# A software-pipelined transformer block on one core: the order of two stages within a step, where they overlap

## The reference

```python
x = x + tanh(g_xattn[0]) * cross_attention_0(layernorm(x), ctx)        # 16 heads of 8, causal
x = x + tanh(g_ffn[0]) * local_transformer(layernorm(x))
x = x + tanh(g_xattn[1]) * cross_attention_1(layernorm(x), ctx)
x = x + tanh(g_ffn[1]) * experts(layernorm(x))                          # top 2 of 8

# local_transformer, twice:
h = shift_token(x); q, k, v = split(h @ wqkv)          # 8 heads of 64, windows of 64
q, k = rotary(l2norm(q) * qs), rotary(l2norm(k) * ks)
x = x + local_attention(q, k, v) @ wo
h = layernorm(shift_token(x)) * lg + lb
a, g = split(h @ w1 + b1)
x = x + (a * gelu(g)) @ w2 + b2
```

## Time and profile before

| what | value |
|---|---|
| median of 3 runs | 1270.78 us (1269.67 to 1273.89) |
| the profiled execution, its own time | 1272.81 us |
| its span | 1270.9 us |
| mean granted clock of PE | 0.96 |

### The profile page before, as it was taken

How to read it: one execution, slowest core, us unless ns; L and a number is a source line. 1 busy time by engine, 2 the same in 40 slices (tenths; PEclk the granted TensorE clock), 3 DMA queues, 4 the chain that set the end, 5 groups by cost and what they waited for, 6 DMA issues and landing times.

```text
span 1270.9 us, 34469 instructions
## 1 busy us (share of the span) xinstructions
PE 1166.9 (92%) x11848; PEld 983.7 (77%) x11848; DVE 1026.1 (81%) x2368; ACT 955.8 (75%) x2545; POOL 859.6 (68%) x1110
## 2 busy tenths in 40 slices
PE   7788976799999998887999999989889998999997
PEld 4377764588888878875888888789767776999997
DVE  3299985899999975677999999858878886688887
ACT  2299984799999985446999999865588986666664
POOL 6188873899999983338999999833576762334332
PEclk8699997999999999998999999999989999999999
DMA  6000000000000001210001200001000000000000
GB/s 181 1 2 2 2 10 7 10 11 10 10 11 10 13 4 23 62 27 8 11 11 27 60 11 13 4 19 31 13 1 1 2 1 2 8 14 13 14 14 13
DMA packets 56555, 21.74 MB, mean 17 GB/s; under 512 B 44689, under 2 KB 54975, under 8 KB 56386
## 3 DMA queue, kind: packets, MB, share of 16 engines
q1 hardware_dynamic: 55154, 19.22, 6.2%
q10 hardware_dynamic: 1232, 0.33, 0.1%
HBM read 9.06 MB, written 2.10 MB: 9 GB/s over the span
## 4 chain that ended last, share of the span: by engine, by line
PE 71%; ACT 8%; DVE 7%; issue 7%; POOL 4%; SPq 1%; DMA 1%; ACTq 0%; DVEq 0%; POOLq 0%
PE m_ps_h L1401 7%; PE m_ps_y L1413 7%; PE a_ps_s L902 5%; PE a_ps_b L994 5%; PE a_ps_t L1005 5%; PE a_ps_t L969 4%; PE a_ps_a L929 4%; PE a_ps_qk L886 3%; PE x_ps_t L575 3%; PE a_ps_s L941 2%; ACT x_khm L636 2%; PE a_ps_qk L888 2%; PE a_ps_qk L887 2%; PE x_ps_s L531 2%; PE f_ps_g L1269 2%
## 5 line engine op out<-in xcount | busy, mean ns | idle before, releaser
L1057 ACT ACTIVATE a_e<-a_ps_s,a_stat 128x128 f32<-128x128 f32 x512 | 226.7, 477 | 4.5 <-DVE a_stat L1126 4.4
L1192 POOL TENSOR_TENSOR a_stat<-a_stat,small 128x16 f32<-128x16 f32 x64 | 187.2, 2925 | 5.3
L1182 POOL TENSOR_TENSOR a_e<-a_e,a_stat 128x1024 f32<-128x1024 f32 x64 | 121.2, 1893 | 8.3 <-DVE a_stat L1105 8.3
L1057 ACT ACTIVATION_READ_ACCUMULATOR a_e<-a_ps_s,a_stat 128x1 f32 x512 | 115.8, 226 | 0.0
L729 DVE TENSOR_REDUCE x_stat<-x_ps_s 128x16 f32<-128x1024 f32 x64 | 78.3, 1224 | 41.2 <-PE x_ps_s L532 41.2
L1299 ACT ACTIVATE f_gl<-f_ps_g,vec 128x128 f32<-128x128 f32 (+1 forms) x192 | 55.8, 361 | 59.7 <-PE f_ps_g L1269 59.6
L1401 PE MATMUL m_ps_h<-m_hT,w 128*128 128x128 f32 x768 | 96.1, 283 | 0.0
L1200 POOL TENSOR_TENSOR a_rot<-a_rot,a_stat 128x512 f32<-128x512 f32 x64 | 90.1, 1407 | 5.0
L1413 PE MATMUL m_ps_y<-w,m_up 128*128 128x128 f32 x768 | 91.1, 275 | 1.5 <-DVE m_yw L1448 1.5
L1401 PEld LDWEIGHTS m_ps_h<-m_hT,w 128*128 128x128 f32 x768 | 90.8, 196 | 0.0
L1434 ACT ACTIVATE m_up<-m_ps_h 128x512 f32<-128x512 f32 x96 | 57.1, 598 | 43.5 <-PE m_ps_h L1401 43.5
(11 more groups left out here) (182 smaller groups left out, 3782.1 us busy)
## 6 DMA issues: line engine op xcount, KB each, us to landing
a_h<-y SPq DMA_DIRECT2D x64, 32.0 KB
f_h<-y SPq DMA_DIRECT2D x64, 32.0 KB
out_dram<-x SPq DMA_DIRECT2D x32, 64.0 KB, 1.5
a_h<-y SPq DMA_DIRECT2D x64, 31.8 KB
f_h<-y SPq DMA_DIRECT2D x64, 31.8 KB
wqkv<-in_L_ffn_wqkv_dram SPq DMA_DIRECT2D x2, 768.0 KB, 5.0
w<-in_L_ffn_w_dram SPq DMA_DIRECT2D x2, 768.0 KB, 5.5
x<-in_x_dram SPq DMA_DIRECT2D x1, 768.0 KB, 5.6
```

What stands on the lines that cost most here:

```text
L1057: act.activation(self.e[n % 2][:, P * i:P * i + P], ps_s[:, P * i:P * i + P], ACT.Exp, bias=stat[:, 24 + i:25 + i], scale=stat[:, root:roo ...
L1182: p.tensor_tensor(e3, e3, self.stat[n % UNROLL][:, 16:24].unsqueeze(2).broadcast_to([P, 8, P]), ALU.mult)\
L1192: p.tensor_tensor(t[:, 48:64], t[:, 32:48], g.neg_half.broadcast_to([P, 16]), ALU.pow).then_inc(self.s_n, 1)
```

## The change

In steps 32 to 42 and 132 to 142 the stages are taken from the oldest to the newest; in all other steps the order stays. Those are the steps in which the first attention and the first local one, and the second local one and its MLP, both have instructions. (`live` only leaves out stages that begin over 15 steps later and so have nothing to write.) The same function serves all five queues.

```diff
         steps = range(-3, start + T + 6)
+
+        def turn(step):
+
+            live = [x for x in stages if x[2] - 15 <= step]
+            for j in (0, 3):
+                if stages[j + 2][2] - 3 <= step < stages[j + 2][2] + 8:
+                    return live
+            return reversed(stages)
+
         block = ctx.enter_context(nc.Block())
 
         @block.sync
         def _(sp):
             for step in steps:
-                for stage, l, start in reversed(stages):
+                for stage, l, start in turn(step):
                     stage.sync(sp, l, step - start)
...
```

## The result

| what | before | changed |
|---|---|---|
| median of 20 runs each | 1270.88 us (1269.19 to 1280.52) | 1265.41 us (1251.85 to 1271.75) |
| the profiled execution, its own time | 1272.81 us | 1260.12 us |
| its span | 1270.9 us | 1258.2 us |
| mean granted clock of PE | 0.96 | 0.965 |

The change makes the kernel faster. The ratio of the times is 0.9929, 95% interval 0.9904 to 0.9953, which is 9.0 us (6.0 to 12.2) or a time of 1261.9 us. The forecast was 1264.6 with a range from 1262.0: the sign is right, the gain came out about 3 us larger, just outside the range.

The account below looks back on a forecast made before the run. No single engine bounds the kernel; POOL sets the pace from 209.96 us in the first overlap. Terms +0.6 − 1.3 − 4.2 − 0.9 − 0.4 = −6.2 us from 1270.78 give 1264.6 us, range 1262.0 to 1268.8.

Parts of the forecast that it names:

- Start of POOL's local work: First overlap: L1189(0) starts near 210.6 against 209.96, 0.6 us later; bounds 1.5 us earlier to 2 us later.
- The walk: First overlap: sum of instruction times from L683 of step 35 at 196.1 to L1189(0), 14.5 us.
- the pieces without a row: First overlap: parts of the 14.5 us sum to L1189(0) without a trace row, estimated from neighbouring steps.
- Roots of step 37 and the waits: First overlap: roots move into POOL's idle time, 1.3 us gained; waits ahead of L1194(1) and L1194(2) go, 4.2 us.
- ACT's y as "what is late next": First overlap, steps 38 to 40: y L617 waits for POOL's roots but is hidden; uncovered, up to 0.5 us a step.
- L1126 and L1182: Second overlap, step 137: L1182 starts earlier, so DVE's L1126 no longer takes 1.07 us beside it; 0.9 us gained.
- The gap ahead of L1258: End of second overlap: PE takes L929 of token 31 before MLP products, covering L1109; 0.4 us gained.
- The slower one: First overlap: local front end waits for the attention's serial chain, L1189(0) 7.8 us late; 1273.1 us; 8%.
- rival 2: Second overlap: the MLP's start sets the end, costing 2.2 us instead of giving 1.3; 1268.1 us; 12%.
- rival 3: First overlap: POOL still waits, as L1164 or PE's lower clock delays rotations; 2.5 us of waits stay; 1267.1 us; 7%.
- Rival 4: The overlaps do not matter: PE, with work that cannot move, sets the pace from 200 us; 1270.8 us; 5%.
- a difference carries over: Whole kernel: the 6.2 us gain worked out on the profiled execution is taken off the 1270.78 us median.

Follow-up runs that it names:

- fillers: Kernel before plus 18 unread PE transposes ahead of L994 of token 30 in both local stages: 1270.36 us, ratio 1.0006.
- D's fillers: Kernel before plus unread PE transposes ahead of the last three L553 and L590 at the second attention's end: 1269.17 us, ratio 0.9973.

## Why the prediction was right and wrong

I take the stretches over all traces. "Old" and "new" mean the order in that stretch's own overlap (in B, which the change doesn't touch, that of the first overlap, all queues).

| stretch | forecast | old order | new order | difference |
|---|---|---|---|---|
| A, L683(27) to L1189(0) | +0.6 | 35.88 (6 traces) | 35.89 (7 traces) | 0.0 |
| A, L1189(0) to L1182(2) | −5.5 | 44.07 (6) | 39.28 (7) | −4.8 |
| C, at a clock of 1.00, with or without fillers | −1.3 | 44.96 (3) | 43.75 (6) | −1.2 |
| C, traces without fillers there that had a lower clock | 0 | 4 of 6, 1.0 us more | 2 of 7, 1.2 and 2.4 us more | −0.2 |
| B, without fillers | 0 | 45.22 (5) | 44.02 (5) | −1.2 |
| end of C to start of D, by C's order, without fillers in C | 0 | 105.70 (6) | 105.11 (7) | −0.6 |

**Start of POOL's local work.** Half right. The forecast said that L683 of step 34 "hardly moves"; it came 2.5 us earlier, 189.60 against 192.10. DVE no longer makes the tables ahead of L683 of step 32, and against the sentence "They take the same time" L1095 itself got shorter:

```profile
179.33 2.23 DVE L1095 TENSOR_TENSOR a_rtab<-c,scl 128x128 f32<-128x128 f32 x4 [0.93 <-issue]
```
```profile
182.91 0.90 DVE L1095 TENSOR_TENSOR a_rtab<-c,scl 128x128 f32<-128x128 f32 x4 [0.66 <-issue]
```

It takes 2.23 to 2.30 us in the six traces with the old order, where it lies beside POOL's x_khm L810 (178.93 to 181.01 in the kernel before), and 0.89 to 0.91 in the eight in which it does not. With POOL's order alone it meets only the end of L810 and takes 1.41 and 1.45. That looks like the collision of L1126 and L1182 once more, but no run isolates it. With the 2.2 us that the forecast did see, L683 of step 35 came at 193.4, not 196.1. The walk from there was too short: L683(31) to L1189(0) took 16.0 us, not 14.5. Up to a_hTr it was right (5.5 us, forecast 5.9). Behind it came the pieces without a row, which took 9.2 to L1115(0) instead of 7.5, with PE at a granted clock of 0.51 from 200 to 210 us, where before it had 0.83. The two errors cancel in part: 0.0 over all traces instead of +0.6.

**Roots of step 37 and the waits.** The mechanism is confirmed by position: three x_st instructions in the gap, no wait ahead of L1194(1). The wait ahead of L1194(2) was named as gone and stayed, 0.94 us in place of 1.02 (0.89 to 1.46 in the seven traces with the new order). I had POOL at about 228.5 and DVE's end at 228.3 to 229, and took the favourable side of a draw. DVE ended at 228.43, but POOL was there at 227.57, since L1189(0) had started 1.1 us ahead of the forecast. What the earlier start won, this wait took back. So that the net for A agrees (−4.8 measured, −4.9 forecast: +0.6, −1.3 and −4.2) is two errors that cancel, and not two terms that were right. The wait's chain runs from L1200(0), which ends at 215.46, over PE's transposes, projections and scores to L969 at 225.48, at first at the lower clock; ACT's y is not on it.

**ACT's y as "what is late next".** Right. Its waits of 3.88, 2.44 and 1.51 us (steps 38 to 40) remain and are hidden. In the kernel without POOL's new order y waits 9.9 to 11.3 us each time with nothing to cover it, and A is 24 us longer.

**L1126 and L1182.** Right in mechanism and size: 1.07 to 0.17 us in every kernel in which POOL takes L1182 ahead of L261, whichever other queue follows, 1.07 to 1.10 in every kernel in which it doesn't, and the same in B (1.04 to 1.10). The Trainium skill's page "SBUF — State Buffer", section "Who interferes with whom", had called it a lock between DVE and GpSimd. By that rule, the trace agrees. The forecast failed to see that the same collision stands in B (L1126 at 467.40 before, 1.07 us), though I had the line's longest duration in the earlier trace rows. It also missed that the new order makes a pair meet that did not meet before: L1126 at 242.03 takes 0.70 us in the changed kernel. That is paid within A.

**The gap ahead of L1258.** It went, with 0.23 us ahead of L1248 in its place, so about 0.2 us of the 0.4.

**Rivals.** The slower one (L1189(0) behind 215) did not come: 204.4 to 212.8 in seven traces. The MLP's start (rival 2) did not bind. Of rival 3, 0.94 of its 2.5 us of waits are there. The slow L1164 that it names is there too, 0.88 to 1.37 us in seven steps between 213 and 278 us, where before three took 0.87 to 1.78; POOL ran without a wait beside them all but for these 0.94 us. Rival 4 is refuted by A.

**What failed** is the step "a difference carries over": it took all else as equal, so the sum lacks a term for PE's clock behind the overlaps and in places that the change doesn't touch. Counted at what the traces show, it is −1.2 us in B, −0.2 in C (4 of 6 traces with 1.0 us more against 2 of 7 with 1.2 and 2.4) and −0.6 between C and D. The last is the clock at the start of the second attention: some 65 us behind the end of C it lies at the lower level for 10.2 us in the kernel before and for 6.8 in the changed one. With these the sum is 0.0 − 4.8 − 1.2 − 1.2 − 0.2 − 0.6 = −8.0 us, against −9.0 (−12.2 to −6.0) by the ratio and −7.4 by the means of all 20 executions. The forecast's −6.2 lies in the ratio's interval too, so a part of the miss may be the draw. The stretch between B and C (307.6 to 309.9 us) varies from trace to trace too widely to be counted. The 12.7 us between the two profiled spans are not the change's size: 2.5 us of them are D, which follows neither order.

**Why B's clock followed the order.** It was 1.00 in all five traces with the new order on all five queues of the first overlap, and fell to between 0.66 and 0.70 in the 5 us from L994 of token 30 in all eight others that have B's order and wait unchanged. The instructions there are the same, and the wait ahead differs by 0.01 us. What does differ is how far that product lies behind the point where the clock last came back to 1.00, at the end of the first overlap: 250.0 to 250.4 us in the five, and 235.4, 240.7, 242.1, 249.6 and 252.0 to 252.6 us in the eight. The same holds in C, where the last rise lies in the start-up of the second local stage. Over both local stages there are 28 such waits without fillers. In 13 the clock stayed at 1.00, at distances of 249.96 to 250.61 us or 240.01 to 240.23; in the other 15 it fell, and none of their distances (235.4, 239.3, 240.7 to 242.1, 249.56 to 249.93, 251.2 to 252.6) lies in these two ranges, though 249.93 and 249.96 are close neighbours. So the gain in B comes of where the new order put this wait behind the clock's last rise. The forecast could not have had that term from the trace of one kernel, but it could have widened its range for it.

**What stays open** is why these distances are the favourable ones. No run here moves the wait by itself. The fillers show that the clock does not fall where the wait is shortened to 0.7 to 0.8 us; one of them stands at a distance of 252.1 us in B, where it fell in four traces without.

## What to carry to other kernels

Where two software pipelines overlap, ask on each in-order queue which stage the others wait for, and put that one first, on every queue that the chain crosses: in one queue alone it can bring the whole gain or cost 24 us. Cost such a change between two milestones of one execution, not between two spans. And put a term for TensorE's clock into the range wherever PE waits a few microseconds, in untouched places too: moving a stall by a microsecond can change the clock behind it.

## What the runs showed that was not expected

The set-up can decide more of one execution's time than the change does. The first L683 starts between 37.67 us (all queues but POOL) and 51.07 us (before, with D's fillers), with the same instructions ahead of it. From 20 to 40 us, the two extremes, columns as in the earlier trace rows:

```profile
20.00:40.00 20.00, 15.63 (x61) 8.07 (x60) 5.18 (x9) 7.07 (x13) 11.43 (x18) 0.95 0.38 107
```
```profile
20.00:40.00 20.00, 19.25 (x50) 10.45 (x49) 0.80 (x3) 2.95 (x6) 10.82 (x15) 0.50 0.37 108
```

At a granted clock of 0.50 PE is busy for 19.25 of 20 us and gets less done (50 against 61 instructions) than at 0.95 in 15.63 us. It waits for only 0.75 us in this stretch, so there is hardly a place for a filler, and no run here tries to change what lies ahead of it. The Trainium skill's page "TensorE: Matmul & The Clock Gate", Part 1, says that the chip's watch on PE's activity doesn't begin with the kernel, so that the point at which the clock changes varies. That fits the differences between executions of the same kernel in C, D and the set-up. In B the level followed the order and not the execution, as the distance to the clock's last rise did.
